# A Mamba-like mixer and a ternary FFN on eight cores: weight passes of w1 and w2 merged, a sum taken from statistics at hand, buffers changed

## The reference, cut to what matters

```python
def attn(x):                       # x: 8 x 4096 x 1024, already layer-normed
    u = x @ W_in.T                                  # 256 states
    gates = silu(x @ W_sel_in.T) @ W_sel_out.T      # 512 hidden, 4 x 256 gates
    a, b, c, dg = sigmoid, tanh, tanh, sigmoid of the four parts
    h[t] = a[t] * h[t-1] + b[t] * u[t]              # scan over the tokens
    return (c * h + d_param * dg * u) @ W_out.T

def act_quant(x):                  # per token, 8 bits
    scale = 127.0 / clip(max(abs(x)), 1e-5)
    return clip(round(x * scale), -128, 127) / scale

def weight_quant(w):               # one scale for the matrix, values -1, 0, 1
    scale = 1.0 / clip(mean(abs(w)), 1e-5)
    return clip(round(w * scale), -1, 1) / scale

def ffn(x):                        # w1: 4096 x 1024, w2: 1024 x 4096
    h = act_quant(x) @ weight_quant(w1).T
    h = silu(depthwise_conv3(h) + conv_b)           # over the tokens
    return act_quant(h) @ weight_quant(w2).T

x = x + layernorm(attn(layernorm(x)))
x = x + layernorm(ffn(layernorm(x)))
```

## Time and profile before

| | |
|---|---|
| median of 2 runs | 3322.31 us (3320.19 to 3324.44) |
| the profiled execution | 3320.45 us |
| its span on the slowest core | 3318.9 us |
| busy: PE, DVE, ACT, POOL | 1559.7, 1514.2, 1222.4, 516.6 us |
| DMA | 260.33 MB, mean 78 GB/s |

### The profile page before, as it was taken

One profiled execution on the slowest core, in us unless ns is written; L12 is line 12 of the kernel. 1 busy time (PEld: TensorE's weight loads), 2 busy tenths in 40 slices (PEclk: granted clock), 3 DMA queues, 4 the chain that ended last, 5 costly groups with the idle time before them and its releaser, 6 DMA issues.

```text
span 3318.9 us, 35433 instructions; the slowest of 8 cores (3303.3 to 3318.9 us)
## 1 busy us (share of the span) xinstructions
PE 1559.7 (47%) x8464; PEld 851.1 (26%) x8464; DVE 1514.2 (46%) x4636; ACT 1222.4 (37%) x1961; POOL 516.6 (16%) x849
## 2 busy tenths in 40 slices
PE   0000023464656465656465656565646564555454
PEld 0000012232323232424232323232323232323130
DVE  1130223736363636363636363636363636364361
ACT  1343333434242424242424242424242424242121
POOL 0000001112121212121202121212121212120101
PEclk9999996667878786868787878686878687877875
DMA  6555630122222222222212222222222221221213
GB/s 186 177 170 177 203 102 20 52 69 64 64 62 66 64 64 64 64 67 61 68 61 64 64 62 66 64 64 61 67 61 67 63 65 51 64 64 51 82 33 102
DMA packets 112699, 260.33 MB, mean 78 GB/s; under 512 B 12656, under 2 KB 12656, under 8 KB 112496
## 3 DMA queue, kind: packets, MB, share of 16 engines
q1 hardware_dynamic: 97808, 212.97, 21.2%
q0 software_dynamic: 10080, 36.70, 3.8%
q10 hardware_dynamic: 4608, 8.39, 0.7%
HBM read 232.85 MB, written 25.17 MB: 78 GB/s over the span
## 4 chain that ended last, share of the span: by engine, by line
DMA 23%; DVE 23%; PE 16%; ACT 11%; DVEq 11%; issue 10%; POOL 2%; ACTq 2%; POOLq 2%; SPq 0%
DMA w2sb<-w2s 14%; DVEq L57 10%; DVE h L834 5%; PE pD L990 5%; DMA stgF<-w1T 4%; DVE h L842 4%; PE pE L990 4%; DVE h L826 3%; PE pE L799 3%; DVE accP L861 2%; DMA stgF<-w2T 2%; DMA w2s<-stgb 2%; POOLq L57 2%; POOL h L974 2%; ACTq L57 2%
## 5 line engine op out<-in xcount | busy, mean ns | idle before, releaser
L990 PE MATMUL pD<-w2sb,h 128*128 128x512 bf16 x1024 | 394.9, 476 | 510.9 <-DMA w2sb<-w2s 379.2
L799 PE MATMUL pE<-xqw,w1t 128*128 128x258 bf16 x4352 | 565.6, 292 | 142.3 <-ACT hpre L808 138.5
L799 PEld LDWEIGHTS pE<-xqw,w1t 128*128 128x128 bf16 x4352 | 449.5, 105 | 253.1 <-issue 163.9
L990 PE MATMUL pE<-w2sb,h 128*128 128x512 bf16 x1024 | 406.0, 488 | 40.1 <-DMA w2sb<-w2s 27.5
L808 ACT ACTIVATE hpre<-pE 128x258 bf16<-128x258 f32 x544 | 184.8, 386 | 509.1 <-DVE h L842 441.6
L974 POOL TENSOR_SCALAR h<-k2i,onec,rccn 128x512 bf16<-128x512 int32 x272 | 229.4, 843 | 604.8 <-ACT k2i L970 558.5
L970 ACT ACTIVATE k2i<-k2f,rcc 128x512 int32<-128x512 bf16 x272 | 193.1, 720 | 341.8 <-DVE k2f L959 264.8
L754 DVE COPY xqw<-xqw 128x8 bf16<-128x8 bf16 x16 | 3.0, 186 | 683.2 <-ACT xqw L747 683.2
L990 PEld LDWEIGHTS pD<-w2sb,h 128*128 128x128 bf16 x1024 | 73.3, 102 | 828.1 <-issue 827.8
L826 DVE TENSOR_SCALAR h<-hpre,cwt,cbt 128x256 bf16<-128x256 bf16 x544 | 186.8, 406 | 116.6 <-ACT hpre L808 103.7
L842 DVE SCALAR_TENSOR_TENSOR h<-hpre,cwt,h 128x256 bf16<-128x256 bf16 x544 | 227.4, 479 | 10.5 <-issue 0.4
(11 more groups left out here) (177 smaller groups left out, 2109.8 us busy)
## 6 DMA issues: line engine op xcount, KB each, us to landing
w2sb<-w2s SPq DMA_DIRECT2D x544, 256.0 KB, 2.6
xin<-x SPq DMA_DIRECT2D x16, 1024.0 KB, 5.2
stgF<-w1T POOLq DMA_DIRECT2D x32, 512.0 KB, 4.0
stgF<-w1T SPq DMA_DIRECT2D x32, 512.0 KB, 4.4
stgF<-w2T POOLq DMA_DIRECT2D x32, 512.0 KB, 4.2
stgF<-w2T SPq DMA_DIRECT2D x32, 512.0 KB, 4.5
out<-stgF SPq DMA_DIRECT2D x32, 512.0 KB, 3.0
w2s<-stgb ACTq DMA_DIRECT2D x16, 256.0 KB, 4.3
```

The source lines that it names most:

```text
L799: lambda e, S, c=c, k=k, off=off, pf=pf: e.matmul(pE[:, off:off + 258], w1t[:, 4096 * k + 128 * c:4096 * k + 128 * (c + 1)], xqv[:, pf, k, :],
L990: coff=coff: e.matmul(bank[:, 512 * jj:512 * (jj + 1)], h4[:, 256 * c + 128 * s:256 * c + 128 * (s + 1)], w2sb[:, coff:coff + 512], start= ...
```

## The change

Four edits.

1. `weight_pass` is gone. Two merged loops take its place: one Abs loop and one quantising loop, in which each of 32 steps handles a piece of w1 and then a piece of w2. The w1 pieces are read as before. The w2 pieces are read by ACT's queue into `tad` and `tbc` (not used before tile 0), under a semaphore "ad" of their own; before each issue the queue waits for the previous one's landing (`q.wait(qn, sem, last_dma[sem])`, which holds for all of these reads). The first two w2 reads are written ahead of the Abs loop. The means of w1 and w2 are then made one after the other. In the quantising loop w1 goes through `k2i` in 1024 columns and w2 through `stgi` in two halves of 512.
2. The ACT pass that summed x2 (L639) and the drain behind it are left out. DVE computes SUM3 = R2 * SUM2 + SUM1 + 1024 * B2 in four operations behind its reductions, and `emit_ln1_prep` gets a wait for them on ACT, since it overwrites SUM1.
3. `stgb` has 2048 columns, one half for each subtile, and POOL's wait for the transpose of subtile 0 (`PE_T2[i][0]`) is left out.
4. `k2f` is left out: DVE multiplies `h4` in place and ACT reads `h4`. DVE's waits for ACT's earlier pairs and its drain (except for pair 0), and POOL's drain, are left out.

```diff
+        c1.queues = (("g", "gd"), ("sy", "sm"))
+        c1.slot = lambda j: stgF[:, 1024 * j:1024 * (j + 1)]
+        c2.queues = (("a", "ad"), ("a", "ad"))
+        c2.slot = lambda j: (tad if j == 0 else tbc)[:, 0:1024]
+        def wp_dma(ctx, p, gate):
+            qn, sem = ctx.queues[p % 2]
+            if gate is None:
+                gate = ctx.gate[p % 2]
+            if gate:
+                q.wait(qn, gate[0], gate[1])
+            q.wait(qn, sem, last_dma[sem])
+            v = q.op(qn, lambda e, S, p=p, ctx=ctx: e.dma_start(
+                out=ctx.slot(p % 2), in_=ctx.src[:, 1024 * p:1024 * (p + 1)]),
+                sem=sem, k=16)
+            last_dma[sem] = v
+            return (sem, v)
...
+        for p in range(32):
+            for ctx in (c1, c2):
+                q.wait("a", *ctx.dmas[p])
                 if p >= 2:
+                    q.wait("a", "dv", ctx.addm[p - 2])
                 q.drain("a")
+                ctx.acm[p] = q.op("a", lambda e, S, p=p, ctx=ctx: e.activation(
+                    ctx.junk, ctx.slot(p % 2), AF.Abs,
+                    accum_out=sc(ctx.acc, p % 2)), sem="ac")
+                ctx.gate[p % 2] = ("ac", ctx.acm[p])
+                if p + 2 < ctx.npc:
+                    ctx.dmas[p + 2] = wp_dma(ctx, p + 2, ("ac", ctx.acm[p]))
...
+            for h in range(2):
+                if p >= 1 or h == 1:
+                    q.wait("a", "dv", ctx.clip[p - 1] if h == 0 else lastc)
+                a_an = q.op("a", lambda e, S, p=p, h=h, ctx=ctx: e.activation(
+                    stgi[:, :], ctx.slot(p % 2)[:, 512 * h:512 * (h + 1)],
...
+            ctx.clip[p] = lastc
+            q.wait("a", "dv", ctx.clip[p])
+            q.wait("a", "swi", max(last_sw))
+            last_sw[p % 2] = q.op("a", lambda e, S, p=p, dstb=dstb: e.dma_start(
+                out=w2s[:, 1024 * p:1024 * (p + 1)], in_=dstb),
+                sem="swi", k=16)
...
-        def emit_ln1_prep(i):
+        def emit_ln1_prep(i, wait_dv=0):
             q.wait("a", *si_x[i])
+            q.wait("a", "dv", wait_dv)
...
                 q.op("a", lambda e, S, s=s, i=i: e.activation(
-                    xin1tm[:, 1024 * s:1024 * (s + 1)], x2s(i, s), AF.Identity,
-                    accum_out=sc("SUM3", s)), sem="ac")
-            q.drain("a")
...
+            q.drain("v")
+            q.op("v", lambda e, S: e.tensor_tensor(
+                sc("QB", 0, 2), sc("R2", 0, 2), sc("SUM2", 0, 2), OP.mult))
...
+            v_sum3 = q.op("v", lambda e, S: e.tensor_tensor(
+                sc("SUM3", 0, 2), sc("QB", 0, 2), sc("QC", 0, 2), OP.add), sem="dv")
+            emit_ln1_prep(i + 1, wait_dv=v_sum3)
...
-                if s == 1:
-                    q.wait("g", "pe", PE_T2[i][0])
...
-                if p2 >= 2:
-                    q.wait("v", "ac", A_anc[f][p2 - 2])
-                elif f > 0:
-                    q.wait("v", "ac", A_anc[f - 1][14 + p2])
-                q.drain("v")
+                    q.drain("v")
...
-                    vtt = q.op("v", lambda e, S, cc=cc, fsl=fsl: e.tensor_tensor(
-                        fsl, h4[:, 256 * cc:256 * (cc + 1)], bc2[:, :], OP.mult),
+                    vtt = q.op("v", lambda e, S, hsl4=hsl4: e.tensor_tensor(
+                        hsl4, hsl4, bc2[:, :], OP.mult),
...
                 q.wait("g", "ac", A_anc[f][p2])
-                q.drain("g")
```

More of the change, by code:

```diff
@@ L239, in build_program @@
         dv_attn_w = stage_cast(woutT, woutT_h, 2 * D)
[L241 to L249, removed]
+        last_dma.update({"ad": 0, "vd": 0})
+        class WP:
+            pass
@@ L250, in weight_pass @@
+        for ctx in (c1, c2):
+            ctx.dmas = [None] * (ctx.npc + 2)
+            ctx.addm = [0] * (ctx.npc + 2)
+            ctx.acm = [0] * (ctx.npc + 2)
+            ctx.dmas[0] = wp_dma(ctx, 0, None)
+            ctx.dmas[1] = wp_dma(ctx, 1, None)
+        for p in range(32):
+            for ctx in (c1, c2):
+                q.wait("a", *ctx.dmas[p])
                 if p >= 2:
-                    q.wait("a", "dv", addmh[p - 2])
+                    q.wait("a", "dv", ctx.addm[p - 2])
@@ L292, in weight_pass @@
[L292 to L302, removed]
+        for ctx in (c1, c2):
+            ctx.dmas = [None] * (ctx.npc + 2)
+            ctx.clip = [0] * (ctx.npc + 2)
+            ctx.dmas[0] = wp_dma(ctx, 0, None)
+            ctx.dmas[1] = wp_dma(ctx, 1, None)
@@ new lines, in build_program @@
+        last_sw = [q.cnt["swi"], q.cnt["swi"]]
+        for p in range(32):
+            ctx = c1
+            q.wait("a", *ctx.dmas[p])
+            if p == 0:
+                q.wait("a", "dv", ctx.vbc)
+            if p >= 1:
+                q.wait("a", "dv", ctx.clip[p - 1])
+            a_an = q.op("a", lambda e, S, p=p, ctx=ctx: e.activation(
+                k2i[:, 0:1024], ctx.slot(p % 2), AF.Identity,
+                scale=wcons[:, ctx.scale_col:ctx.scale_col + 1],
+                bias=rcc[:, 0:1]), sem="ac")
+            ctx.gate[p % 2] = ("ac", a_an)
+            if p + 2 < ctx.npc:
+                ctx.dmas[p + 2] = wp_dma(ctx, p + 2, ("ac", a_an))
+            q.wait("v", "ac", a_an)
+            dstb = w1t[:, 1024 * p:1024 * (p + 1)]
+            q.drain("v")
+            q.op("v", lambda e, S, dstb=dstb: e.tensor_scalar(
+                dstb, k2i[:, 0:1024], -RC, -1.0, OP.add, OP.max))
+            q.drain("v")
+            ctx.clip[p] = q.op("v", lambda e, S, dstb=dstb: e.tensor_scalar(
+                dstb, dstb, 1.0, None, OP.min), sem="dv")
+            ctx = c2
+            q.wait("a", *ctx.dmas[p])
+            if p == 0:
+                q.wait("a", "dv", ctx.vbc)
+            dstb = stgb[:, 0:1024] if p % 2 == 0 else selh[:, 0:1024]
+            lastc = 0
+            for h in range(2):
[3 more added lines that the diff above has]
+                    stgi[:, :], ctx.slot(p % 2)[:, 512 * h:512 * (h + 1)],
+                    AF.Identity,
+                    scale=wcons[:, ctx.scale_col:ctx.scale_col + 1],
@@ L303, in weight_pass @@
                     bias=rcc[:, 0:1]), sem="ac")
-                stg_gate[p % 2] = ("ac", a_an)
-                if p + 2 < npc:
-                    dmas[p + 2] = piece_dma(p + 2, src_h, ("ac", a_an))
+                if h == 1:
+                    ctx.gate[p % 2] = ("ac", a_an)
+                    if p + 2 < ctx.npc:
+                        ctx.dmas[p + 2] = wp_dma(ctx, p + 2, ("ac", a_an))
                 q.wait("v", "ac", a_an)
[L308 to L313, removed]
+                if h == 0 and p >= 2:
+                    q.wait("v", "swi", last_sw[p % 2])
@@ L320, in weight_pass @@
[L320 to L329, removed]
+                lastc = q.op("v", lambda e, S, dsl=dsl: e.tensor_scalar(
+                    dsl, dsl, 1.0, None, OP.min), sem="dv")
```

121 lines of the change are left out of this document (69 added, 52 removed).

## The result

The changed kernel takes 3327.1 us in the median, the kernel before 3320.2 us in the runs beside it. The ratio is 1.0019, with a 95% interval of 1.001 to 1.0028: a little slower, by 6 us or 0.2%, where 53 us less were forecast. In the profiled execution the slowest core is core 0, with a span of 3323.0 us at a mean granted clock of 0.784; before it was core 4, with 3318.9 us at 0.797.

What follows compares the result with a forecast made beforehand. No single engine was taken as the bound: setup passes wait for pieces to land, tiles for a chain through L421. Terms -81 + 33 + 1 - 6 = -53 us gave 3268 us, range 3236 to 3300.

Steps and rivals of the forecast that it cites:

- part 3: Pairs before L618: multiplying in place without POOL's drain starts L618 0.4 us earlier in tiles 1 to 15, 6 us.
- part 4: Subtile transposes in each tile: doubling stgb and dropping POOL's wait gains nothing, since ACT's order still holds it.
- Pairs 6 to 15 run in the DMA-bound stretch: nothing: Later pairs of a tile: the w2sb reads cover them, so multiplying in place without POOL's drain gains nothing there.
- L: Merged Abs loop: latency of a 512 KB w2 read on ACT's queue, taken as 4.4 us, giving 4.46 us steps.
- the forecast's ladder: Setup: step-by-step sum of both merged loops, putting LN1 of tile 0 at 376.4 instead of 457.3 us, 81 us gained.
- A: Setup: single w2 reads on ACT's queue land in 3.5 us, 26 us less, 3242 us; chance 0.2.
- B: Setup: transfers are full, more reads slow each; 12 us gained against 28 lost, 3336 us; chance 0.09.
- C: Quantising loop: stores stand behind reads on ACT's queue, a 6.6 us step, 26 us more, 3293 us; chance 0.15.
- D: Tiles: the wait for SUM3 before the next LN1 is hidden, no 34 us lost, 3234 us; chance 0.07.

Runs made afterwards that it cites:

- the run with two semaphores: Changed kernel with w2's reads counted on two semaphores by turns, so two w2 reads are in flight: ratio 0.9941 to the kernel before.
- the first experiment: Changed kernel with ACT summing x2 again and DVE's four SUM3 operations and the wait before the next LN1 removed: ratio 0.9916 to the kernel before.

## Why the prediction was wrong

The prediction of 3268 us and its range, 3236 to 3300 us, missed 3327. Its own sum was -81 for edit 1, +33 and +1 for edit 2, -6 for edit 4 and nothing for edit 3. Measured were about -60 (-63 in the run with edit 1 alone), +34, +36 and nothing. The prediction numbers its parts in another order than the list of edits: its part 3 is edit 4, its part 4 is edit 3.

**Edit 4, the step that failed.** "DVE no longer waits for ACT in pairs 1 to 5": this was priced as a small gain, 0.4 us a tile, with bounds of nothing and 0.8 us, all on the side of a gain. The bounds left out that the removed waits had also spaced DVE's products, and that POOL works at the same time. The traces showed that POOL's first conversion lasts until DVE's run of products is over: 3.25 us instead of 0.96 at pair 6, 1.62 at pair 0 and 5.67 in the last two windows. "Pairs 6 to 15 run in the DMA-bound stretch: nothing" was wrong for the first of them, pair 6, for which PE is already idle, although the prediction had said exactly that of pair 6 in the part on edit 2. Pair 0 and pair 6 together account for 2 us in each of fifteen tiles (0.5 at chunk 0, 1.5 at chunk 12), 30 us, and the last two windows for 5 us each (PE's idle before chunk 0 there is 8.5 instead of 3.6 us). That is up to 40 us; undoing the edit gave 36, and putting back the waits for ACT alone gave 45. With the forecast gain of 6 this is a term mis-sized by 42 us, and with the wrong sign; it alone takes the time out of the range (3268 + 42 = 3310 us), which the 20 us of edit 1 would not have done.

The Trainium skill has the rule that should have been a rival here: SBUF — State Buffer, section "Who interferes with whom", says that a DVE operation with two inputs in SBUF and a GpSimd operation that reads SBUF exclude each other, the second one waiting in full. The trace agrees that POOL's conversion is held. It goes further than the sentence: POOL waits out not one product but twenty that follow each other without a gap. That a shared port is the reason is the skill's statement; the runs show the dependence on DVE's run and nothing of the port itself.

**Edit 1, right in kind, too large by 20 us.** The Abs step is set by ACT's wait for the previous w2 read, as forecast, and the run with two semaphores confirms it. L was taken as 4.4 us and came out at 4.5 and 4.7 us for w2's reads (4.7 and 5.2 for w1's), near the upper bound of 4.7. These are its DMA issues between 60 and 180 us:

```profile
tad<-w2T ACTq DMA_DIRECT2D x13, 512.0 KB, 4.7
tbc<-w2T ACTq DMA_DIRECT2D x12, 512.0 KB, 4.5
```

The Trainium skill, DMA: Bandwidth & Descriptors, section "Anatomy of one DMA", from which the prediction took 3.2 us, gives its fit for DMAs that GpSimd issues. Here those are only POOL's reads of w1, at 4.7 us in the same window, so the trace does not agree for them either.

From the first to the last w2 Abs it took 143.5 us (196.52 - 53.05) instead of the 135 us that the forecast's ladder gives (184.6 - 49.6): 8.5 us. The prefetch of two w2 pieces, costed at nothing, delayed the casts (the second one starts at 20.28 instead of 17.43 us) and so the first Abs from 48.4 to 51.8 us: 3.5 us. The gap between the loops was 7.7 us instead of 6.2: the w2 read issued at 196.67 us takes 7.0 us to land. Why this one takes longer than the others, no run shows. The quantising step was 6.02 us instead of 5.8: 7 us over 32 steps; the timeline has 5.97 us from L343 to L343 even where no read is issued:

```profile
384.77 1.24 ACT L343 ACTIVATE k2i<-stgF,rcc,wcons 128x1024 int32<-128x1024 f32 x1 [1.58 <-DVE selh L384]
385.92 0.80 ACT L367 ACTIVATE stgi<-tad,rcc,wcons 128x512 int32<-128x512 f32 x1
388.35 0.81 ACT L367 ACTIVATE stgi<-tad,rcc,wcons 128x512 int32<-128x512 f32 x1 [1.64 <-DVE stgb L384]
390.25 0.33 ACTq L389 DMA_DIRECT2D w2s<-stgb  x1
390.74 1.24 ACT L343 ACTIVATE k2i<-stgF,rcc,wcons 128x1024 int32<-128x1024 f32 x1 [1.58 <-DVE stgb L384]
```

The ladder is the one of the prediction, with the second half 0.1 us and the store 0.15 us later than the estimated clips gave. Together 8.5 + 3.5 + 1.5 + 7 = 20.5 us.

**Edit 2, right.** Forecast 33 us and 1, measured 34; L487 comes 5.74 us after the start of the pass over the second x2, where 5.7 us follow from the forecast's 1462.95 us.

**Edit 3, right.** Nothing forecast, nothing measured.

**The rivals.** A (quick reads, 3.5 us) is refuted: 4.5 to 4.7 us. B (full transfers) is refuted for the changed kernel: 221 GB/s in the Abs loop where 179 were moved before, and 257 with a further read in flight. The rule of the Trainium skill that spoke for it (DMA: Bandwidth & Descriptors, section "Issuing engines are not separate DMA queues"), that queues share the same engines, is not contradicted: what was used is idle share, and the share went from 0.55 to 0.75. (B's own steps, 32 x 5.9 and 32 x 6.6 us, end the setup at 448 us, 9 us gained and not 12.) C (stores) is refuted too: a step is 6.0 us, where C had 6.6, and the stores take 4.0 and 4.5 us in the median, where C needed 6.5. D (the sum's wait hidden) is refuted by the first experiment. The time ended close to B's, 3336 us, by none of these ways: that is chance.

## What to carry to other kernels

A wait that is taken out may have paced an engine that gets in another's way: before costing it at nothing, look at what the freed engine will do in one go and who works beside it, above all in front of a wait that sets the end. When an engine's pass is replaced by a few cheap operations on another, write them where that engine is idle, not behind its queue; the same four operations made +34 us in one place and -34 us in the other. And a buffer gives nothing while the program's own order still waits for the old one: look at which engine stands behind the event in its queue.

## What the runs showed of the hardware that was not expected

- POOL's int32 to bf16 conversion of 128 x 512, 0.77 to 1.02 us otherwise, ends 0.64 to 0.66 us after the end of a run of DVE tensor-tensor products of 128 x 256 bf16, for runs of 12, 20 and 32 products (2.5, 4.1 and 6.6 us). When the products come in groups of four or two, as when DVE waits for ACT, a conversion takes some 0.25 us longer at most.
- With up to three 512 KB reads in flight a core moved 221 GB/s at a DMA share of 0.75; with up to four, on another chip, 257 GB/s at 0.84. The reads' median time to landing was 4.5 to 5.2 us in the first case and 5.7 to 7.0 us in the second.
